# Second experts' rows added into the output by an adding scatter, in place of a scatter, a reload and a gated sum

## The chip, the cores and the metric

One NeuronCore of a Trainium2 chip runs the whole program. The metric is the device time in microseconds of one execution. The engines are TensorE (PE in the profile), VectorE (DVE), ScalarE (ACT), GpSimd (POOL) and SyncE (SP, which only issues DMAs). A row that begins with SPq, ACTq or POOLq is an instruction of that engine's sequencer.

## The reference, cut to what matters

The network has two graph layers and two mixture-of-experts layers over 1250 nodes of 512 features. Only the last layer is touched:

```python
f = layernorm(x)                              # 1250 x 512
logits = f @ Wr                               # 8 experts
top_vals, top_idx = top_k(logits, 2)
gates[n, top_idx[n]] = softmax(top_vals)[n]
for e in range(8):
    y = gelu(f @ W1[e] + b1[e]) @ W2[e] + b2[e]
    out = out + gates[:, e:e+1] * y
result = x + out
```

So each node's result is its row of x plus two expert rows, each times a gate of its own.

## The kernel before, in words

Rows of x are held in the chip's memory as 10 tiles of 125 partitions (node 125 t + p is partition p of tile t). Up to line 1721 the kernel computes x, adds the graph layer to it (line 1340 on POOL, one tile at a time, semaphore `conv_added`), normalises it into `T.rows_b` (line 1713 on ACT, `f_rows`), and turns it for the router's products. SP stores the normalised rows into the DRAM tensor `rows1` in groups of 4, 4 and 2 tiles: the first two groups at line 1272, the last by POOL at line 1342. In `rows1` partition p has its 10 rows next to each other.

DVE then makes the routing (lines 1891 to 1956). The 2500 pairs of node and choice are sorted by expert into blocks of 128 places, 28 blocks at most, and 24 are in use with these inputs. `rows_placed` (803) and L1926 make 0/1 matrices, and PE multiplies them with numbers of nodes (`make_numbers`, 812) and with the choice, first or second (`make_choices`, 820). From these DVE makes `T.ids` (the node of each place, 1937) and `T2.sids` (the row of the DRAM tensor `y1` that each place's result goes to, 1939 to 1943). `keep_busy` (123) issues products whose results nobody uses, 24 of them at 1609 and 24 at 1616.

Then come the blocks, in the functions `block_turn`, `block_hidden`, `turn_hidden`, `block_output`. For block r:

- POOL copies a column of ids (1310) and gathers 128 rows of `rows1` by an indirect DMA (1316), one of 4 buffers. It copies a column of `sids` (1313) and scatters the results of block r-4 into `y1` (1326). It issues these in one order, gather r, then scatter r-4, with a wait for `ry_copied` between.
- PE turns the gathered rows (1527), multiplies with W1 of the block's expert (1535), turns the result (1544), multiplies with W2 (1552). The order on PE is: turn hidden r-1, hidden r, turn of block r+1, output r-1.
- DVE adds b1 (1856), copies the turned rows (1850), adds b2 into `T.ry` (1863), one of 4 buffers.
- ACT takes the gelu (1694) and copies its turned result (1699).

The first 4 blocks and the last 4 stand alone, those between are a loop of 4 to a turn. Scatter r waits only until its buffer's next user is free, so several are in flight. The last 4 count on `ry_last`.

After the last scatter has landed, SP loads `y1` back in 10 DMAs (1277): place p, tile t, first and second choice. DVE does `x = x + gate * row` 20 times (1966, 1968), and ACT stores x into `out` in 10 DMAs (1743) and waits for them. `y1` has rows that no node owns, and lines 880 to 883 fill them once, much earlier, from SP.

Of the kernel before, what the change touches and what calls it, by code (L numbers as in the profile page):

```python
# [815 lines left out]

def make_choices(pe, T, bank, rows, place, columns):
# [52 lines left out]
def projections(nc, T, S, A):  # L870


    with nc.Block() as block:

        @block.sync
        def _(sp):
# [3 lines left out]
            for j in range(TOP):  # L880
                spare = A.y1[j * PLACES + NT * P:(j + 1) * PLACES].rearrange("(p t) d -> p (t d)", t=NT)
                for c0, c1 in ((0, KD * N), (KD * N, NT * D)):
                    sp.dma_start(spare[:, c0:c1], feats[0:128 - P, 0:c1 - c0]).then_inc(S.rows_filled, 16)
            for j in range(TOP):
# [3 lines left out]
            sp.wait_ge(S.rows_filled, 128)  # L888
# [270 lines left out]
def routed_layers(nc, T, T2, S, A):  # L1159
# [62 lines left out]
    with nc.Block() as block:  # L1222

        @block.sync
        def _(sp):
# [55 lines left out]
        @block.gpsimd  # L1281
        def _(pool):
# [59 lines left out]
            pool.dma_start(A.rows1.rearrange("(p t) d -> p t d", t=NT)[:, NT - 2:], T.rows_b[:, NT - 2:]).then_inc(S.tail_stored, 16)  # L1342
            pool.wait_ge(S.ids_ready, 2)
            pool.wait_ge(S.table_made, 2 * TOP)
# [914 lines left out]
```

## Time and profile before

| what | value |
|---|---|
| median of 3 runs | 1360.15 us (1358.65 to 1361.75) |
| profiled execution, its time | 1373.4 us |
| profiled execution, its span | 1371.7 us |
| PE, DVE, ACT, POOL busy | 96%, 54%, 34%, 26% of the span |
| mean granted clock of TensorE | 0.972 |

The span runs from the first to the last instruction of the profiled execution, and all times in rows are microseconds from its start. The profiled execution is 13.25 us (1.0%) above the median. PE's 96% is an average over many stages; it says nothing of the last 25 us, in which PE does nothing.

### The profile page before, as it was taken

What the parts mean: (1) busy time and instruction counts of PE and PEld (TensorE: products, weight loads), DVE (VectorE), ACT (ScalarE), POOL (GpSimd) and SP (SyncE); (2) the same over time, 40 slices, a digit from 0 to 9 for tenths busy, and PEclk for the clock granted to TensorE, in tenths of its full rate; (3) what the DMA queues carried; (4) which work ended last, traced back from release to release, by engine and by line L of the source; (5) the groups of instructions that cost most, each with busy time, mean ns of one, the idle gap of its engine ahead of it and who ended that gap; (6) DMA issues with size and microseconds to landing.
All of it is one profiled execution on the core that took longest, in us unless ns stands there. A gap on an engine that the chain in (4) does not pass through costs nothing.

```text
span 1371.7 us, 23245 instructions
## 1 busy us (share of the span) xinstructions
PE 1316.7 (96%) x7745; PEld 881.9 (64%) x7746; DVE 736.0 (54%) x1600; ACT 461.9 (34%) x1152; POOL 350.6 (26%) x491
## 2 busy tenths in 40 slices
PE   9999999999989999999998999999999999899991
PEld 4799954455457777777656777777645555666660
DVE  6799955562158888887575333333352011453334
ACT  2699921011045555555312111111332012521110
POOL 4499920000000000000033555555200000314540
PEclk9999999999999999999999999999999999769996
DMA  6000000040010000000242999999420070312326
GB/s 166 32 2 3 2 1 1 0 188 0 0 42 2 1 2 2 2 1 2 69 139 85 338 329 319 316 322 311 156 115 0 0 245 0 129 53 88 104 85 237
DMA packets 83549, 133.32 MB, mean 97 GB/s; under 512 B 11952, under 2 KB 49222, under 8 KB 82687
## 3 DMA queue, kind: packets, MB, share of 16 engines
q1 hardware_dynamic: 69491, 110.29, 24.6%
q0 software_dynamic: 12176, 18.68, 4.4%
q10 hardware_dynamic: 1788, 3.16, 0.7%
q8 instruction: 52, 0.85, 0.3%
q14 instruction: 42, 0.34, 0.1%
HBM read 117.41 MB, written 29.56 MB: 107 GB/s over the span
## 4 chain that ended last, share of the span: by engine, by line
PE 45%; DVE 3%; DMA 1%; issue 1%; ACT 0%; SPq 0%; POOL 0%; POOLq 0%; DVEq 0%
PE ps L1377 8%; PE ps L1386 8%; PE ps L1469 6%; PE ps L1535 3%; PE ps L1552 3%; PE ps L1519 2%; PE ps L1514 2%; PE ps L123 2%; PE ps L1367 1%; PE ps L1571 1%; PE ps L1486 1%; PE ps L1412 1%; DMA b_r<-y 1%; PE ps L1527 1%; PE ps L1464 1%; PE ps L164 1%
## 5 line engine op out<-in xcount | busy, mean ns | idle before, releaser
L1298 POOL TENSOR_TENSOR b_x<-b_x,b_r 125x512 f32<-125x512 f32 x10 | 12.7, 1271 | 526.5 <-DVE b_r L1769 526.5
L1377 PEld LDWEIGHTS ps<-b_r 128*128 128x128 f32 x1024 | 124.2, 192 | 33.7 <-issue 32.2
L1377 PE MATMUL ps<-b_r 128*128 128x78 f32 x1024 | 122.2, 272 | 1.2 <-DVE b_r L1751 1.2
L1386 PE MATMUL ps<-b_r 128*78 128x512 f32 x256 | 120.3, 592 | 0.0
L659 PE MATMUL ps<-b_r 125*125 125x160 f32 x660 | 117.3, 314 | 0.1
L568 ACT ACTIVATE b_r<-b_r 125x125 f32<-125x125 f32 x330 | 106.8, 390 | 0.4 <-issue 0.2
L1651 ACT ACTIVATE b_r<-ps,b_r 128x78 f32<-128x78 f32 x128 | 34.8, 323 | 203.0 <-PE ps L1377 196.7
L1047 PEld LDWEIGHTS ps<-b_r 125*64 125x64 f32 x1600 | 85.3, 136 | 24.6 <-issue 22.8
L1010 PE MATMUL ps<-b_r 64*125 64x417 f32 (+1 forms) x480 | 95.7, 531 | 1.4 <-DVE ps L1139 1.2
L1047 PE MATMUL ps<-b_r 125*64 125x125 f32 x1600 | 94.7, 272 | 1.3 <-ACT b_r L1075 1.3
L659 PEld LDWEIGHTS ps<-b_r 125*125 125x125 f32 x660 | 92.0, 187 | 5.4 <-ACT b_r L568 0.2
L1757 DVE COPY b_r<-ps 78x512 f32<-78x512 f32 x64 | 44.0, 687 | 81.1 <-PE ps L1386 78.7
L1469 PE MATMUL ps<-b_r 125*128 125x417 f32 (+1 forms) x240 | 87.3, 513 | 0.0
L676 PE MATMUL ps<-b_r 125*125 125x512 f32 x200 | 86.2, 593 | 0.7 <-DVE b_r L474 0.7
L1292 POOL DMA_INDIRECT y<-b_r,b_affine x64 | 62.0, 969 | 97.1 <-DVE b_r L1757 97.1
L1070 DVE COPY b_r<-ps 125x500 f32<-125x500 f32 x120 | 77.7, 676 | 5.9 <-PE ps L1017 0.7
L1751 DVE COPY b_r<-ps 128x312 f32<-128x312 f32 x64 | 30.9, 483 | 87.4 <-PE ps L1377 52.9
L1286 POOL DMA_INDIRECT b_r<-rows,b_ids x64 | 66.4, 1038 | 28.0 <-issue 18.6
L460 DVE TENSOR_TENSOR b_r<-ps,b_r 125x480 f32<-125x480 f32 x110 | 72.0, 655 | 0.5 <-PE ps L659 0.2
L1083 ACT ACTIVATE b_r<-ps,b_neg_max 125x1251 f32<-125x1251 f32 x40 | 52.2, 1304 | 59.1 <-DVE b_neg_max L1113 55.9
L676 PEld LDWEIGHTS ps<-b_r 125*125 125x125 f32 x200 | 37.4, 188 | 48.3 <-issue 48.3
L1469 PEld LDWEIGHTS ps<-b_r 125*128 125x128 f32 x240 | 44.4, 189 | 36.1 <-issue 35.2
(286 smaller groups left out, 2305.6 us busy)
## 6 DMA issues: line engine op xcount, KB each, us to landing
b_r<-L_ffn_w SPq DMA_DIRECT2D x128, 512.0 KB
b_r<-y SPq DMA_DIRECT2D x20, 512.0 KB, 7.7
b_r<-L_ffn_W SPq DMA_DIRECT2D x2, 4096.0 KB, 20.0
y<-b_r SPq DMA_DIRECT2D x2, 2500.0 KB
rows<-b_r SPq DMA_DIRECT2D x4, 960.0 KB
b_x<-x SPq DMA_DIRECT2D x5, 480.0 KB
out<-b_x ACTq DMA_DIRECT2D x5, 480.0 KB
b_r<-L_ffn_b SPq DMA_DIRECT2D x1, 2048.0 KB, 8.9
```

Source lines behind the costliest of these rows:

```text
L460: dve.tensor_tensor(T.cells[:, b], cell_iota.unsqueeze(1).to_broadcast([EC, CJ, WC]), column(T.cell_col, g, WC), ALU.is_equal).then_inc(S. ...
L568: last = act.activation(T.weighted[:, i % 2, j, :], T.sources[:, i % 2, j, :], ACT.Copy, scale=T.w_col[:, bass.ds(g0 + i, 1), j])
L659: last = pe.matmul(T.ps[:P, 2 + b, 0:WC], T.weighted[:, b, j, :], T.cells[:, b, j, :], start=(j == 0), stop=(j == CJ - 1))
L676: last = pe.matmul(T.ps[:P, t % 2, :], T.at[:, k, t * P:(t + 1) * P], T.rows_a[:, k, :], start=(k == 0), stop=(k == NT - 1))
L1010: last = pe.matmul(T.ps[:P, 3 * h + c, 0:width], T.qt[b:b + DH, m, t * P:(t + 1) * P], T.kt[b:b + DH, m, c0:c0 + width], start=True, stop= ...
L1047: last = pe.matmul(T.ps[b:b + DH, bank_of((VALUES, n)), 0:P], T.v[:, k, m * 128 + b:m * 128 + b + DH], T.probs_t[:, n % 2, h, k * P:(k + 1 ...
L1070: copy(T.probs_t[:, n % 2, h, t * P:(t + 4) * P], bank).then_inc(emptied, 1)
L1286: pool.indirect_dma_start(T.ex[:CAP, e % SLOTS, :], None, A.rows0, bass.IndirectOffsetOnAxis(ap=T.ids[:CAP, e:e + 1], axis=0), bounds_chec ...
L1292: pool.indirect_dma_start(A.y0, bass.IndirectOffsetOnAxis(ap=T.sids[:CAP, e:e + 1], axis=0), T.ey[:CAP, e % SLOTS, :], None, bounds_check= ...
L1377: last = pe.matmul(T.ps[:, 2 + r % 2, f * CAP:(f + 1) * CAP], T.ew1[r % WS][:, k, f * 128:(f + 1) * 128], T.ex_t[:, r % 2, k, :], start=(k ...
L1386: last = pe.matmul(T.ps[:CAP, 4 + r % 2, :], T.eh[:, r % 2, f, :], T.ew2[r % WS][:, f, :], start=(f == 0), stop=(f == FK - 1))
L1469: return pe.matmul(T.ps[:, bank_of(j), 0:n], T.rows_a[:, k, m * 128:(m + 1) * 128], T.ct_f[:, k, c0:c0 + n], start=(k == 0), stop=(k == NT ...
```

## The change

The result of a block is multiplied by its places' gates on DVE, and scattered with an add straight into `out`, which by then holds x. Two choices of one node are in different blocks, and two adds to one row must not overlap, so each scatter waits until the one before it has landed.

- x is stored into `out` by SP, in the same three groups as the normalised rows and between them: x group 0, rows group 0, x group 1, rows group 1, x group 2 (6 DMAs added).
- `rows1` is stored by node number (node 125 t + p at row 125 t + p), so one list of ids serves the gather and the scatter. `make_choices` and four steps of DVE go.
- Gates per place: DVE splits the gates into three bf16 parts (`split_gates`, before the ids), spreads them over the place matrix (`gates_placed`, 3 instructions of 560 elements, after the ids), PE makes 20 products of 84 columns (`make_gates`), DVE adds the parts (`slot_gates`, 3 instructions). PE's second filler is 10, then the gates, then 6, where it was 24.
- In the blocks DVE has one more instruction, a multiplication of 128x512 in place, which waits for the one before it (`ry_copied`), and POOL waits for `ry_scaled`, then for the landing of the scatter before.
- The reload, DVE's 20 instructions and ACT's 10 stores at the end go, as do the four fills of `y1`. SP waits for the last scatters at the end.
- The place matrices move from region r1 to r2, so that they outlive the first gathers.

```diff
-            for j in range(TOP):
-                spare = A.y1[j * PLACES + NT * P:(j + 1) * PLACES].rearrange("(p t) d -> p (t d)", t=NT)
-                for c0, c1 in ((0, KD * N), (KD * N, NT * D)):
-                    sp.dma_start(spare[:, c0:c1], feats[0:128 - P, 0:c1 - c0]).then_inc(S.rows_filled, 16)
...
-            for t0, n in GROUPS[:2]:
+            for t0, n in GROUPS:
+                sp.wait_ge(S.conv_added, t0 + n)
+                for p0, p1 in ((0, 120), (120, P)):
+                    sp.dma_start(A.out.rearrange("(t p) d -> p t d", t=NT)[p0:p1, t0:t0 + n], T.x[p0:p1, t0:t0 + n])\
+                      .then_inc(S.out_stored, 16)
+                if t0 + n == NT:
+                    break
                 sp.wait_ge(S.f_rows, t0 + n)
                 for p0, p1 in ((0, 120), (120, P)):
-                    sp.dma_start(A.rows1.rearrange("(p t) d -> p t d", t=NT)[p0:p1, t0:t0 + n], T.rows_b[p0:p1, t0:t0 + n])\
+                    sp.dma_start(A.rows1.rearrange("(t p) d -> p t d", t=NT)[p0:p1, t0:t0 + n], T.rows_b[p0:p1, t0:t0 + n])\
                       .then_inc(S.rows_stored, 16)
+            sp.wait_ge(S.out_stored, 96)
             sp.wait_ge(S.ry_last, 64)
-            for i in range(NT // 2):
-                for j, rows in enumerate((T.all_a, T.all_d)):
-                    sp.dma_start(rows[:, 2 * i:2 * i + 2],
-                                 A.y1[j * PLACES:(j + 1) * PLACES].rearrange("(p t) d -> p t d", t=NT)[:, 2 * i:2 * i + 2])\
-                      .then_inc(S.y_gathered[i], 16)
...
-                if r + 1 < 8:
-                    wait_count(pool, S.ry_stored[(r + 1) % 4], q, 16, 16 * ((r + 1) // 4))
-                pool.wait_ge(S.ry_copied, q * 4 + (r + 1))
+                pool.wait_ge(S.ry_scaled, q * 4 + (r + 1))
+                if r > 4:
+                    pool.wait_ge(S.ry_last, 16 * (r - 4))
+                else:
+                    wait_count(pool, S.ry_stored[(r + 3) % 4], q, 16, 16 if r > 0 else 0)
                 place_column(q, r + 1, (r + 1) % 4 if r + 1 < 8 else 4)
-                pool.indirect_dma_start(A.y1, bass.IndirectOffsetOnAxis(ap=T.ey_ids[:, r % 4:r % 4 + 1], axis=0),
-                                        T.ry[:, r % 4, :], None, bounds_check=TOP * PLACES - 1, oob_is_err=False)\
+                pool.indirect_dma_start(A.out, bass.IndirectOffsetOnAxis(ap=T.ey_ids[:, r % 4:r % 4 + 1], axis=0),
+                                        T.ry[:, r % 4, :], None, bounds_check=N - 1, oob_is_err=False, compute_op=ALU.add)\
                     .then_inc(stored, 16)
...
-            pool.wait_ge(S.table_made, 2 * TOP)
             token_column(0, 0)
...
-            make_choices(pe, T2, 3, BR, T2.place, NB).then_inc(S.table_made, 1)
-            keep_busy(pe, T, 0, 24)
+            keep_busy(pe, T, 0, 10)
+            pe.wait_ge(S.gates_ready, 2)
+            make_gates(pe, T2, 5).then_inc(S.table_made, 1)
+            keep_busy(pe, T, 0, 6)
...
+                dve.wait_ge(S.ry_copied, q * 4 + (r + 1))
+                dve.tensor_scalar(T.ry[:, r % SLOTS1, :], T.ry[:, r % SLOTS1, :], T2.slot_gate[:, bass.ds(q * 4 + r, 1)], None,
+                                  ALU.mult).then_inc(S.ry_scaled, 1)
...
             gates(dve, link, T)
+            split_gates(dve, link, T2)
             dve.wait_ge(S.table_made, 1 + TOP)
...
+            link(dve.tensor_scalar(T2.sids[:, 0:NB], T.ps[:BR, 7, 0:NB], float(N), None, ALU.add))
             dve.tensor_copy(T.ey_ids[:, 0:1], T2.sids[:, 0:1])
+            gates_placed(dve, T2, S.gates_ready)
...
             block_turned(0, 0)
+            dve.wait_ge(S.table_made, 2 + TOP)
+            slot_gates(dve, link, T2, 5)
             end = blocks(dve, block_step)
             block_output(*end)
-
-            rows = (T.rows_a, T.rows_d)
-            for t in range(NT):
-                dve.wait_ge(S.y_gathered[t // 2], 64)
-                link(dve.scalar_tensor_tensor(out=T.x[:, t, :], in0=rows[0][:, t, :], scalar=T.gate[:, t, 0:1],
-                                              in1=T.x[:, t, :], op0=ALU.mult, op1=ALU.add))
-                dve.scalar_tensor_tensor(out=T.x[:, t, :], in0=rows[1][:, t, :], scalar=T.gate[:, t, 1:2],
-                                         in1=T.x[:, t, :], op0=ALU.mult, op1=ALU.add).then_inc(S.out_ready, 1)
```

The new functions:

```python
def split_gates(dve, link, T):
    rest = T.gate[:]
    for i in range(3):
        link(dve.tensor_copy(T.split[:, i], rest))
        if i < 2:
            link(dve.tensor_tensor(T.rest[:], rest, T.split[:, i], ALU.subtract))
            rest = T.rest[:]

def gates_placed(dve, T, ready):
    for i in range(3):
        last = dve.tensor_tensor(T.gate_parts[:, :, :, i, :], T.place[:],
                                 T.split[:, i].rearrange("p t j -> p j t").unsqueeze(3).to_broadcast([P, TOP, NT, NB]), ALU.mult)
    last.then_inc(ready, 1)
```

## Rows read from the trace of the kernel before

**Rows 1.** Windows of the block stage, of the reload's start and of the end.
```profile
core 0: us, PE busy (x) PEld busy (x) DVE busy (x) ACT busy (x) POOL busy (x), PEclk, DMA share, GB/s
1232.00:1345.00 113.00, 106.67 (x442) 69.45 (x439) 41.22 (x72) 19.27 (x48) 56.49 (x93) 1.00 0.28 91
1345.00:1352.00 7.00, 0.00 (x0) 0.00 (x0) 0.00 (x0) 0.00 (x0) 0.67 (x1) 0.50 0.57 197
1352.00:1372.00 20.00, 0.00 (x0) 0.00 (x0) 14.41 (x20) 0.00 (x0) 0.00 (x0) 0.50 0.86 323
```

**Rows 2.** The chain that ended last, its last pieces: start, us, what.
```profile
1336.06 1.99 PE ps L1535 x8
1340.56 1.99 PE ps L1552 x4
1344.68 2.28 DMA y<-b_r
1351.76 12.88 DMA b_r<-y
```

**Rows 3.** Timeline of the last block: start, us, instruction, idle before it.
```profile
1341.59 0.99 POOL L1326 DMA_INDIRECT y<-b_r  x1 [0.55 <-issue]
1342.69 0.69 DVE L1863 TENSOR_TENSOR b_r<-ps,b_r 128x512 f32<-128x512 f32 x1 [2.08 <-PE ps L1552]
1343.93 0.18 POOL L1313 COPY b_r<-b_r 128x1 int32 x1 [1.36 <-DVE b_r L1863]
1344.68 0.99 POOL L1326 DMA_INDIRECT y<-b_r  x1 [0.57 <-issue]
1346.98 5.33 SPq L1277 DMA_DIRECT2D b_r<-y  x10
```

**Rows 4.** The scatters of the block stage, by line: durations, first and last start, landing.
```profile
L1326 POOL DMA_INDIRECT y<-b_r x24: 982/1026/1035, 1245.4 to 1344.7; - x24
DMA to landing us min/median/max: 2.1/2.5/2.8
```

**Rows 5.** Windows around the last scatter, then around a gather issued at 1239.05.
```profile
1344.68:1345.67 0.99, 0.00 (x0) 0.00 (x0) 0.00 (x0) 0.00 (x0) 0.99 (x1) 0.63 0.00 0
1345.67:1346.20 0.53, 0.00 (x0) 0.00 (x0) 0.00 (x0) 0.00 (x0) 0.00 (x0) 0.50 0.00 0
1346.20:1347.00 0.80, 0.00 (x0) 0.00 (x0) 0.00 (x0) 0.00 (x0) 0.00 (x0) 0.50 0.16 47
...
1239.05:1240.70 1.65, 1.33 (x7) 1.13 (x7) 0.00 (x0) 0.38 (x1) 1.02 (x1) 1.00 0.00 0
1240.70:1241.40 0.70, 0.70 (x6) 0.57 (x5) 0.00 (x0) 0.00 (x0) 0.00 (x0) 1.00 0.44 118
1241.40:1242.15 0.75, 0.75 (x7) 0.51 (x6) 0.56 (x2) 0.10 (x1) 0.00 (x0) 1.00 0.08 33
```

**Rows 6.** DVE in a middle block, from the timeline, and normalisation's multiply by line.
```profile
1327.21 0.69 DVE L1863 TENSOR_TENSOR b_r<-ps,b_r 128x512 f32<-128x512 f32 x1 [1.15 <-issue]
1329.41 0.42 DVE L1856 TENSOR_TENSOR b_r<-ps,b_w_b 128x256 f32<-128x256 f32 x1 [1.51 <-PE ps L1535]
...
L216 DVE TENSOR_SCALAR b_r<-b_x,b_moments,b_rstd x30: 545/545/547, 7.9 to 1039.1; 125x512 f32<-125x512 f32 x30
```

**Rows 7.** Timeline of the routing on DVE, PE and POOL.
```profile
1223.05 0.81 DVE L1926 TENSOR_TENSOR b_r<-b_block_iota,b_keep 125x280 f16<-125x280 f32 x2
1227.25 0.17 DVE L710 TENSOR_TENSOR b_gate<-b_gate,b_gap 125x10 f32<-125x10 f32 x1
1228.63 0.19 DVE L1937 TENSOR_SCALAR b_ids<-ps 128x28 int32<-128x28 f32 x1 [1.21 <-PE ps L812]
1228.62 5.34 PE L123 MATMUL ps<-b_ones_bf 125*128 125x512 bf16 x24
1230.37 1.10 POOL L1316 DMA_INDIRECT b_r<-rows,b_ex_ids  x1 [0.92 <-issue]
1234.01 0.63 PE L1527 MATMUL ps<-b_ident,b_r 128*128 128x128 f32 x4
```

**Rows 8.** Windows between the stores of rows1 and the first gather.
```profile
1199.00:1210.00 11.00, 11.00 (x49) 9.61 (x49) 3.16 (x11) 3.24 (x7) 0.63 (x1) 0.50 0.50 126
1216.00:1220.00 4.00, 4.00 (x37) 4.00 (x37) 2.19 (x17) 0.21 (x1) 0.00 (x0) 0.50 0.00 0
1234.00:1236.00 2.00, 1.01 (x6) 0.76 (x7) 0.69 (x1) 0.00 (x0) 1.02 (x3) 1.00 0.68 213
```

**Rows 9.** SP's waits over the whole run: us in total, times, longest.
```profile
SPq L873 <- PEq L873: 86.6, 1, 86.6
```

More of the change, by code:

```diff
@@ L814, in make_numbers, with make_gates, slot_gates @@
     return last
+def split_gates(dve, link, T):
+    rest = T.gate[:]
+    for i in range(3):
+        link(dve.tensor_copy(T.split[:, i], rest))
+        if i < 2:
+            link(dve.tensor_tensor(T.rest[:], rest, T.split[:, i], ALU.subtract))
[4 more added lines that the diff above has]
+                                 T.split[:, i].rearrange("p t j -> p j t").unsqueeze(3).to_broadcast([P, TOP, NT, NB]), ALU.mult)
+    last.then_inc(ready, 1)
+def make_gates(pe, T, bank):
+    for t in range(NT):
+        for j in range(TOP):
+            last = pe.matmul(T.ps[:BR, bank, 0:3 * NB], T.place_rows[:, t * TOP + j, :],
+                             T.gate_parts[:, j, t].rearrange("p i b -> p (i b)"),
+                             start=(t + j == 0), stop=(t == NT - 1 and j == TOP - 1))
+    return last
+def slot_gates(dve, link, T, bank):
+    part = [T.ps[:BR, bank, i * NB:(i + 1) * NB] for i in range(3)]
+    link(dve.tensor_copy(T.slot_gate[:], part[2]))
+    link(dve.tensor_tensor(T.slot_gate[:], part[1], T.slot_gate[:], ALU.add))
+    link(dve.tensor_tensor(T.slot_gate[:], part[0], T.slot_gate[:], ALU.add))
 def make_choices(pe, T, bank, rows, place, columns):
@@ L887, in _ @@
                     sp.dma_start(filled[:, c0:c1], feats[:, 0:c1 - c0]).then_inc(S.rows_filled, 16)
[L888 removed]
+            sp.wait_ge(S.rows_filled, 64)
         @block.tensor
@@ L1341, in _ @@
             pool.wait_ge(S.f_rows, NT)
-            pool.dma_start(A.rows1.rearrange("(p t) d -> p t d", t=NT)[:, NT - 2:], T.rows_b[:, NT - 2:]).then_inc(S.tail_stored, 16)
+            pool.dma_start(A.rows1.rearrange("(t p) d -> p t d", t=NT)[:, NT - 2:], T.rows_b[:, NT - 2:]).then_inc(S.tail_stored, 16)
             pool.wait_ge(S.ids_ready, 2)
-            pool.wait_ge(S.table_made, 2 * TOP)
             token_column(0, 0)
@@ L1350, in _ @@
             pool.wait_ge(S.blocks_ready, 1)
+            pool.wait_ge(S.out_stored, 96)
             loops = loops_of(pool)
@@ L1737, in _ @@
             block_turned(*end)
-            out = A.out.rearrange("(t p) d -> p t d", t=NT)
-            for i in range(NT // 2):
-                act.wait_ge(S.out_ready, 2 * i + 2)
-                for p0, p1 in ((0, 120), (120, P)):
-                    act.dma_start(out[p0:p1, 2 * i:2 * i + 2], T.x[p0:p1, 2 * i:2 * i + 2]).then_inc(S.out_stored, 16)
-            act.wait_ge(S.out_stored, 16 * NT)
         @block.vector
@@ L1890, in _ @@
             one, other = T.expert_iota[:, 0:E1].unsqueeze(1), T.expert_iota[:, 0:E1].unsqueeze(2)
-            link(dve.scalar_tensor_tensor(out=T2.place_number, in0=T.part_number[:].to_broadcast([P, NT]), scalar=float(NT),
-                                          in1=T.tile_iota[:], op0=ALU.mult, op1=ALU.add))
-            link(dve.tensor_scalar(T2.place_number, T2.place_number, float(NOWHERE - N), None, ALU.add))
+            link(dve.scalar_tensor_tensor(out=T2.place_number, in0=T.tile_iota[:], scalar=float(P),
+                                          in1=T.part_number[:].to_broadcast([P, NT]), op0=ALU.mult, op1=ALU.add))
+            link(dve.tensor_scalar(T2.place_number, T2.place_number, float(EMPTY - N), None, ALU.add))
             dve.memset(T2.sids[:, NB:], 0)
@@ L1935, in _ @@
             gates(dve, link, T)
+            split_gates(dve, link, T2)
             dve.wait_ge(S.table_made, 1 + TOP)
             dve.tensor_scalar(T.ids[:, 0:NB], T.ps[:BR, 7, 0:NB], float(N), None, ALU.add).then_inc(S.ids_ready, 1)
-            low, place = T.ids_low[:, 0:NB], T2.place_ids[:, 0:NB]
-            link(dve.tensor_scalar(low, T.ps[:BR, 7, 0:NB], float(N), None, ALU.add))
-            link(dve.tensor_scalar(place, low, float(N), float(TOP * PLACES), ALU.is_ge, ALU.mult))
-            link(dve.tensor_tensor(place, place, low, ALU.add))
-            dve.wait_ge(S.table_made, 2 * TOP)
-            link(dve.scalar_tensor_tensor(out=T2.sids[:, 0:NB], in0=T.ps[:BR, 3, 0:NB], scalar=float(PLACES), in1=place,
-                                          op0=ALU.mult, op1=ALU.add))
+            link(dve.tensor_scalar(T2.sids[:, 0:NB], T.ps[:BR, 7, 0:NB], float(N), None, ALU.add))
             dve.tensor_copy(T.ey_ids[:, 0:1], T2.sids[:, 0:1])
+            gates_placed(dve, T2, S.gates_ready)
             last_block = T.first_block[:P, E1:E1 + 1]
```

13 lines of the change are left out of this document (8 added, 5 removed).

## The prediction

> **What bounds the kernel now.** The windows come first, because the page's 96% for PE is an average. In the block stage PE is busy 106.67 of 113 us at the full clock (1.00, the 2.4 GHz level), and from 1345 to the end it does nothing [rows 1]. So two stages matter: one in which PE sets the pace, and one in which only DVE and DMAs work. The chain that ended last says the same: PE's products up to 1342.54, then the last scatter, then 12.88 us of reloads and what follows them [rows 2]. The last scatter is issued at 1344.68, and 2.28 us later SP's reload starts, at 1346.98 [rows 2, 3]. The span ends at 1371.7. The tail after the last landing is therefore 1371.7 - 1347.0 = 24.7 us. All 24 scatters start between 1245.4 and 1344.7, and the first 23 of them take 1341.59 - 1245.4 = 96.2 us, 4.37 us from one to the next [rows 3, 4]. That is PE's pace. The last gap is 3.09 us, since PE has no further block by then [rows 3].
>
> **What goes.** The reload, the 20 gated sums and the stores: all of the 24.7 us, in which nothing else runs. The four fills of y1 save nothing: SP waited 86.6 us for PE at the end of that stage, so four DMAs fewer leave it waiting longer [rows 9].
>
> **The stores of x.** Six more DMAs, 2.5 MB, go through SP's queue ahead of and between the stores of normalised rows, and the first gather has to wait for the latter. The stores of rows1 moved 126 GB/s over 11 us up to 1210, in a stage where engines and not DMAs set the pace; 2.5 MB at that rate take 20 us. Group 0 of x is ready when POOL has added four tiles, long before its normalised rows, and the stretch from 1216 to 1220 has no DMA at all [rows 8]. The gather is issued at 1230.37 [rows 7]. I cost the stores at nothing; the cover is that idle stretch. If they were late, the gather would slip by what is left of them, a few us at most. The new order in rows1 keeps the bytes and makes pieces of 2 KB out of 8 KB; the same cover holds.
>
> **The routing.** DVE gets five linked steps of some 0.2 us each before the ids (the last step of the gates takes 0.17), 1.05 us in all, and it sat idle 1.21 us there for PE [rows 7]. So they fit with nothing much to spare; I take +0.1 us. After the ids, four steps go (0.9 us with their gaps) and one comes (0.2). The three spreads of 560 elements are priced from the 280-element comparison, 0.405 us each: at most twice that, 0.8 us, so 2.4 us together [rows 7]. The gates' products can start near 1231.5. PE's filler of 10 takes 10 x 0.222 = 2.2 us (24 took 5.34) from about 1228.4, PE idles about 1 us, the 20 products take about 1 us, the filler of 6 takes 1.3: PE is free at 1233.8, where before it was at 1233.96 [rows 7]. The first gather lands some 3 us after its issue anyway. Net: 0 to +0.3, I take +0.1. DVE's list of block experts is ready near 1232.7, before the first turn at 1234.01. `slot_gates` (3 x 0.2 us) fits behind the first copy, while PE makes the first hidden product.
>
> **The blocks on DVE.** The multiplication costs 0.55 us, the time of the 125x512 row that also multiplies by a column (a lower price is possible with one operation less, none below 0), and 0.05 for its wait: 0.6 us. It stands between L1863, which ends at 1327.90, and L1856 at 1329.41, an idle of 1.51 us [rows 6]. PE waits for `ry_copied`, which comes before it. So it costs PE nothing and makes each scatter ready 0.6 us later. The first is issued at 1245.4 + 0.6 = 1246.0.
>
> **One scatter at a time.** This decides the change. POOL now waits for the landing of the scatter before, copies a column and issues. From the start of that copy to the next scatter it takes 0.75 us (1343.93 to 1344.68), and I add 0.2 for POOL waking before the copy, 0.95 us [rows 3]. With L for the time from an adding scatter's issue to its landing, one scatter follows another at L + 0.95 at the soonest. PE's pace of 4.37 hides that up to L = 3.42. Above it, a chain from the first scatter sets the end: last issue = 1246.0 + 23 (L + 0.95), last landing L later, and about 0.6 us to the span's end. **End = 1268.4 + 24 L.** Each tenth of a us in L is 2.4 us.
>
> No row shows an adding DMA, so L is bounded from its parts. A plain scatter lands after 2.1 to 2.8 us, the last one after 2.28 [rows 2, 4]; adding can't be quicker, as it writes the same rows and reads more. That is the lower end, 2.3. In the windows the scatter moves nothing for 1.5 us and then works for 0.8; a gather, which reads such rows from DRAM, moves nothing for 1.6 us and then works for up to 1.4 [rows 5]. If an adding scatter did the whole of a gather and then the whole of a scatter's part behind the issue (2.5 - 1.0 = 1.5), it would be 3.1 + 1.5 = 4.6, and with the longest scatter and some more for the issue of extra descriptors 5.0. That is the upper end. I take 1.6 us to the first packet, 1.2 for the reads at a gather's pace and 0.7 for the writes at a scatter's: L = 3.5, nearer to the lower end because reads and writes of different rows can overlap.
>
> The Trainium skill (DMA: Bandwidth & Descriptors, "Two DMAs through the same engine are not ordered") says that only the completion semaphore orders a DMA behind one that writes what it reads; it is why the wait is there, and it speaks against this change. The same page ("Anatomy of one DMA — SWDGE (gpsimd) path") puts about 2.0 us plus bytes / 436e3 on a DMA; for 256 KB that is an estimate of 2.6 us, near the rows' 2.5, and by it alone the add would be hidden.
>
> **The sum.** End = 1268.4 + 24 x 3.5 = 1352.4, plus 0.1 for the routing: 1352.5 against 1371.7, a gain of 19.2 us. The profiled execution lies 1.0% above the median of the runs; I take the same gain off the median: 1360.15 - 19.2 = **1341.0 us**.
>
> **Rivals.**
>
> *All of it hidden.* If only the data phase grows by the 0.7 us of a second read, L is 3.1 and PE keeps the pace. The last scatter but one goes out at 1342.2, the last at 1342.2 + 3.1 + 0.95 = 1346.3, and the end is at 1350.0, a gain of 21.7: 1338.5 us. With L = 2.3 the gain is 23.4 and the time 1336.8. For it: the plain scatter's 16 queues work for only 0.8 us. Against: the gather's reads are slower than the scatter's writes in the same windows. The Trainium skill (Collectives: The Full Stack, "The bandwidth ceiling: the fold count and why AG ≠ RS ≠ AR") holds that an adding DMA is slower because of its two source reads and not because of the add; that is this case.
>
> *The chain of landings becomes the bound and eats the gain.* Place: POOL's wait for the landing before L1313's copy. It decides from L = 4.30, where 1268.4 + 24 L is 1371.7. At the upper end of 5.0 the end is at 1388.4, 16.7 us later: 1376.9 us. Gathers then queue behind the waiting POOL and PE starves at POOL's pace. For it: reads of DRAM followed by writes of the same rows leave no room for overlap within a row, and the descriptors of an add may take POOL longer than 1.0 us to issue. Against: eight rows per queue can follow each other. This is the case on the other side.
>
> *The clock.* PE's filler is shorter and has a gap of about 1 us. If the granted clock fell to 0.50 there, some 4 us of PE's work would take twice as long, +2 us. Against: it held 1.00 in a stretch of which PE worked only 1.01 of 2.00 us [rows 8]. It changes no sign.
>
> **How the numbers follow.** A measurement of this kernel can tell about 0.2% (2.7 us) from no change. In L the bounds of "same" are 4.19 and 4.41. Chances: L up to 3.2, all hidden, 0.24 (1337 to 1339); L from 3.2 to 4.19, the forecast's case, 0.42 (1339 to 1357); L within the bounds of "same", 0.07; L above, 0.27 (1363 to 1377 and more). That makes faster 0.66, same 0.07, slower 0.27. The range takes both ends of L: 1336 from the plain scatter's time, and 1377 from 5.0. The forecast's side alone is 1336 to 1357.
>
> **What would show it.** In the profile after: the landing of the adding scatters by line (3.5 us); their distance from one to the next (4.45, against 4.37); POOL's wait before L1313's counterpart put down to a DMA and not to DVE; the span ending within 1 us of the last landing; the first turn of block 0 within 0.3 us of 1234.0; the clock at 1.00 from 1226 on; DVE's multiplication at 0.55 us with PE's time per block unchanged. It is wrong if the landing is above 4.3 us, or if PE's first turn slips by more than 1 us.

## The result, and the profile after

The change makes the kernel slower: 1373.93 us (median of 4 runs, 1371.46 to 1381.96) against 1360.95 (4 runs, 1358.65 to 1362.24), a ratio of 1.0109 with a 95% interval of [1.0071, 1.0146]. A second measurement gave 1371.49 (13 runs) against 1361.46 (23 runs), 1.0059 [1.0036, 1.0083]. So it costs 10 to 13 us where 19 were forecast to be won. 1373.9 lies inside the range of 1336 to 1377, but on the other side of no change from the forecast of 1341.0, in the part that the second rival held.

TensorE's mean granted clock differs from one execution to the next, in both kernels: the profiled execution of before was at 0.972, the first profiled one of the changed kernel at 0.985, its second (the same kernel, experiment 8) at 0.977. In both kernels an execution with the lower mean (0.972 to 0.974 before, 0.977 changed) takes some 12 us more than the others, and the profile of before is one of these. The windows show where. First the kernel before, then the changed kernel's first and second execution; the third figure from the end is the granted clock:

```profile
1190.00:1200.00 10.00, 10.00 (x46) 9.21 (x45) 4.50 (x18) 4.79 (x10) 0.00 (x1) 0.50 0.42 109
1200.00:1210.00 10.00, 10.00 (x44) 8.61 (x43) 3.16 (x11) 3.24 (x7) 0.63 (x1) 0.50 0.47 119
1210.00:1225.00 15.00, 14.44 (x74) 10.84 (x74) 9.62 (x62) 3.36 (x9) 0.00 (x0) 0.50 0.03 12
```

```profile
1190.00:1200.00 10.00, 9.84 (x80) 8.13 (x79) 7.17 (x28) 7.40 (x16) 0.00 (x0) 1.00 0.89 259
1200.00:1210.00 10.00, 8.46 (x72) 7.06 (x72) 6.44 (x53) 2.14 (x4) 1.23 (x1) 0.79 0.44 139
1210.00:1225.00 15.00, 12.63 (x87) 6.48 (x86) 10.99 (x37) 3.71 (x11) 5.85 (x9) 0.91 0.19 55
```

```profile
1190.00:1200.00 10.00, 10.00 (x47) 9.30 (x46) 4.11 (x17) 4.42 (x9) 0.00 (x0) 0.50 0.72 210
1200.00:1210.00 10.00, 10.00 (x45) 8.61 (x43) 3.16 (x11) 3.23 (x7) 1.23 (x1) 0.50 0.54 144
1210.00:1225.00 15.00, 14.44 (x73) 10.57 (x73) 10.04 (x63) 3.77 (x11) 0.00 (x0) 0.50 0.08 27
```

Before and the second execution both did these 35 us at 0.50, the 1.2 GHz level; the first did most of them at 1.00. I therefore set the second execution (span 1382.2, time 1383.92) against the profile of before (span 1371.7, time 1373.4). That is 10.5 us, as the medians say, and the stages in front of the change hardly differ. In the first execution the first scatter is issued at 1234.1 and not at 1245.5; these 11 us go with the clock and not with the change. What makes the clock come out one way or the other isn't shown.

The scatters by tile, second execution (durations, first and last start, who waited, landing), with two windows, from the first scatter to the last and from there to the end:

```profile
L1362 POOL DMA_INDIRECT out<-b_r x24: 1563/1594/1636, 1245.5 to 1375.2; - x24
who waited for it (us, times):
  POOL b_r L1347: 42.7, 21
DMA to landing us min/median/max: 3.4/4.8/5.0
```

```profile
1245.50:1375.24 129.74, 98.96 (x384) 59.91 (x382) 50.12 (x89) 17.59 (x44) 65.33 (x84) 0.97 0.41 70
1375.24:1382.20 6.96, 0.00 (x0) 0.00 (x0) 0.00 (x0) 0.00 (x0) 1.56 (x1) 0.50 0.05 7
```

Against [rows 1, 4]: an issue takes 1.59 us where it took 1.03, a landing 4.8 where it took 2.5, and between first and last scatter PE works 98.96 of 129.74 us, so it is no longer the bound. (The 2.5 is the median of the only four landings that the trace of before has, and two of these blocks were nearly empty; the other two landed after 2.7 to 2.8 us.) The chain that ended last says what is: from 1245.48 on its long pieces are landings of this kind, with POOL's copy and issue between them, and its last piece is POOL's closing drain. Three of these pieces:

```profile
1341.98 4.97 DMA out<-b_r
1369.17 4.76 DMA out<-b_r
1375.02 1.79 POOLq L1254
```

The timeline of POOL and of the engines that feed it, same execution, one block:

```profile
1341.98 1.59 POOL L1362 DMA_INDIRECT out<-b_r  x1 [0.59 <-POOL b_r L1347]
1343.94 1.06 POOL L1350 DMA_INDIRECT b_r<-rows,b_ex_ids  x1 [0.16 <-issue]
1345.96 0.49 DVE L1897 TENSOR_SCALAR b_r<-b_r 128x512 f32<-128x512 f32 x1
1347.17 0.18 POOL L1347 COPY b_r<-b_r 128x1 int32 x1 [2.17 <-DMA out<-b_r]
1347.94 1.60 POOL L1362 DMA_INDIRECT out<-b_r  x1 [0.59 <-POOL b_r L1347]
1348.07 0.66 PE L1563 MATMUL ps<-b_ident,b_r 128*128 128x128 f32 x4 [1.23 <-DMA b_r<-rows,b_ex_ids]
```

The scaled rows were ready at 1346.45, 0.5 us before the scatter of 1341.98 landed (at 1346.95). POOL starts its copy 0.22 us after that landing and the next scatter 0.77 later, 5.96 us behind the last. The gather stands behind the scatter in POOL's queue, so PE waits 1.23 us for gathered rows and works at POOL's pace.

The description of the kernel before says that several of its scatters are in flight. They may be, but [rows 4] shows that they weren't: they were issued 4.3 us apart and landed within 2.8.

**The balance**, predicted and measured, in us of these executions:

| term | before | predicted | measured |
|---|---|---|---|
| first scatter issued at | 1245.4 | 1246.1 | 1245.5 |
| first to last scatter, 23 distances | 99.3 | 102.4 (4.45 each) | 129.8 (5.64 each) |
| last scatter to the end of the span | 27.0 | 4.1 | 6.9 |
| span | 1371.7 | 1352.5 | 1382.2 |

The tail gives 20.1 us back and the distances take 30.5, 10.5 in all with the 0.1 of the first term. Of the error of 29.7 us, 27.4 lie in the distances and 2.8 in the end; the first scatter came 0.6 earlier than forecast.

**The end** is a part of its own. The closing drain, an instruction with which each engine ends the program, is no busy time; it stands by the line of the block that ends the program. In the kernel before, then in the changed kernel's first execution (with what SP did) and its last scatter from POOL's timeline:

```profile
L1222 POOLq DRAIN  x1: 6353/6353/6353, 1344.5 to 1344.5; - x1
```

```profile
L1254 POOLq DRAIN  x1: 6932/6932/6932, 1362.6 to 1362.6; - x1
L1254 SPq DRAIN  x1: 13/13/13, 1366.4 to 1366.4; - x1
L1254 SPq EVENT_SEMAPHORE  x1: 17/17/17, 1369.7 to 1369.7; - x1
```

```profile
1362.78 1.56 POOL L1362 DMA_INDIRECT out<-b_r  x1 [0.89 <-issue]
```

SP saw the last landing and was through at 1366.4; then all waited 3.3 us for POOL. The last scatter's issue ends at 1362.78 + 1.56 = 1364.34, and the drain at 1362.56 + 6.93 = 1369.49, 5.14 us behind it. In the kernel before it ended 5.14 us behind the end of the last issue as well (1345.67, 1350.81), but there it lay beside the reload and cost nothing. The change took that cover away.

### The profile page after: what moved, and what is told of

It reads as the page before. It is cut to its first block, busy times and chain, and to the rows that moved or that the text cites. A ratio compares the mean times of both kernels' runs of the same rounds, so it can differ in the third digit from the quotient of the medians.

```text
span 1369.7 us, 23259 instructions
## 1 busy us (share of the span) xinstructions
PE 1306.6 (95%) x7747; PEld 870.3 (64%) x7748; DVE 736.9 (54%) x1612; ACT 461.2 (34%) x1152; POOL 366.5 (27%) x491
## 4 chain that ended last, share of the span: by engine, by line
PE 35%; DMA 8%; DVE 4%; issue 2%; POOL 1%; ACT 1%; POOLq 0%; DVEq 0%
PE ps L1413 8%; PE ps L1422 8%; DMA out<-b_r 7%; PE ps L1505 6%; PE ps L1555 2%; PE ps L1550 2%; PE ps L1403 1%; PE ps L1522 1%; PE ps L1448 1%; PE ps L1439 1%; PE ps L1500 1%; PE ps L123 1%; DVE b_stats L200 1%; PE ps L144 1%; DMA b_r<-rows,b_ex_ids 1%
## 6 DMA issues: line engine op xcount, KB each, us to landing
b_r<-L_ffn_W SPq DMA_DIRECT2D x2, 4096.0 KB, 20.1
```

## Experiments

Twelve runs: eleven edits of the changed kernel, and the changed kernel itself again. Where "one execution" is said, the time is a single one and says little within some us. "Distance" is the mean of the 23 from first to last scatter in the profiled execution, "end" is from the last scatter's issue to the span's end.

### 1. The scatter without its add

```diff
-                    T.ry[:, r % 4, :], None, bounds_check=N - 1, oob_is_err=False, compute_op=ALU.add)\
+                    T.ry[:, r % 4, :], None, bounds_check=N - 1, oob_is_err=False)\
```

> The changed kernel with a plain scatter in place of the adding one; every wait stays. The rows of x are overwritten, so the output leaves out the sum. Theory (the landing of the adding scatter is the cost: 4.8 us from issue to landing, 5.8 us from one scatter to the next): a plain scatter lands after about 2.5 us, the chain asks for 3.4 us, PE's 4.37 us sets the pace again, and the time falls by about 24 x 1.4 = 33 us, to some 1340 us. Rival (the longer routing, the multiplication on DVE, the stores of x or the wait itself cost the time, whatever lands): the distance between scatters stays near 5.8 us and the time near 1372 us. Second rival (the issue of 1.6 us on POOL is the cost, and it is the same with indices into the output): the issue stays at 1.6 us.

1339.13 us (ratio to before 0.9833 [0.9777, 0.989]).

```profile
L1362 POOL DMA_INDIRECT out<-b_r x24: 985/1021/1034, 1235.7 to 1331.9; - x24
DMA to landing us min/median/max: 2.1/2.8/3.3
```

Distance 4.18, end 6.4, issue 1.0: the theory held against both rivals. Everything else of the change is in this kernel: the stores of x between those of the rows, the gates, the wait for each landing. So these together cost next to nothing, and the add costs 32 to 35 us. The time is also within a us of what the first rival gave for a hidden landing (1338.5), but in part by luck: in this execution the end is 2.7 us longer than that rival had it (3.7), and the distances together are 4.1 us shorter (96.2 against 100.3).

### 2. The column copied before the waits

```diff
+                place_column(q, r + 1, (r + 1) % 4 if r + 1 < 8 else 4)
                 pool.wait_ge(S.ry_scaled, q * 4 + (r + 1))
...
-                place_column(q, r + 1, (r + 1) % 4 if r + 1 < 8 else 4)
+                pool.sem_inc(S.pool_go, 1)
```

The last line counts up a semaphore that nobody waits for; the wait for the landing stands at this instruction.

> POOL copies the column of places before it waits for the landing, not between landing and issue. Theory: the distance between scatters is landing plus 0.95 us now and becomes landing plus about 0.3 us, so 23 x 0.65 = 15 us go: 1358 us, level with the kernel before. Rival (POOL's own work of gather, copies and issue sets the pace, and the order of its steps doesn't matter): the distance stays within 0.1 us of 5.8 and the time within 3 us of 1373.

1370.49 us (1.0074 [1.0037, 1.011]), 1 to 3 us less than the changed kernel where 15 were expected: a miss. The rival, that POOL's own work sets the pace, isn't borne out either: experiment 3 has the same work and a distance of 4.2.

```profile
1256.46 1.60 POOL L1363 DMA_INDIRECT out<-b_r  x1 [2.57 <-DMA out<-b_r]
1262.09 1.59 POOL L1363 DMA_INDIRECT out<-b_r  x1 [2.39 <-DMA out<-b_r]
```

The distance is 5.54 against 5.6, though no copy stands between landing and issue. From a landing to the next issue it is 0.84 to 0.90 us here and was 0.93 to 1.01 with the copy (1.32 at the last scatter). So nearly all of it is POOL's own way from a semaphore to a started indirect DMA, and the copy, which takes 0.18, runs mostly inside it. My theory had the 0.65 us as the copy's.

### 3. Two chains

Even blocks add into `out`, odd ones into a second tensor, and a scatter waits for the one before last. The sum of the two tensors is left out.

```diff
-                if r > 4:
-                    pool.wait_ge(S.ry_last, 16 * (r - 4))
+                if r > 5:
+                    pool.wait_ge(last_of[r % 2], 16)
...
-                    wait_count(pool, S.ry_stored[(r + 3) % 4], q, 16, 16 if r > 0 else 0)
+                    wait_count(pool, S.ry_stored[(r + 2) % 4], q, 16, 16 if r > 1 else 0)
...
-                pool.indirect_dma_start(A.out, ...
+                pool.indirect_dma_start((A.out, A.y1)[r % 2], ...
```

> Blocks of even number add into the output, blocks of odd number into a second tensor, and each scatter waits for the one before the last. The odd blocks' sums are left out of the output. Theory (latency of one scatter behind another): two may be in flight, a chain asks for (4.8 + 0.95) / 2 = 2.9 us per block, PE sets the pace at 4.37 us and the time is near 1340 us. Rival (the adding scatters are bound by what the queues can do at all, so two in flight take twice as long each): landings of 7 us or more, a distance of over 5 us and a time over 1355 us.

1337.88 us (0.9826 [0.9772, 0.9881]). From the DMA view (issues, median us to landing):

```profile
out<-b_r POOLq DMA_INDIRECT x12, 4.8
y<-b_r POOLq DMA_INDIRECT x12, 4.8
```

The kernel is as quick as without the add. The adds' work isn't the bound, nor is their issue of 1.6 us; waiting for one before the next is. How far two adds can share the DMA engines is not shown: the distance here is 4.2 us, and a scatter's data moves from 2.1 to 4.5 us behind its issue (windows under "Why the prediction was wrong"), so one add has moved its data before the next begins.

### 4 and 5. Half the columns, half the places

```diff
-                pool.indirect_dma_start(A.out, bass.IndirectOffsetOnAxis(ap=T.ey_ids[:, r % 4:r % 4 + 1], axis=0),
-                                        T.ry[:, r % 4, :], None, bounds_check=N - 1, oob_is_err=False, compute_op=ALU.add)\
+                pool.indirect_dma_start(A.half, bass.IndirectOffsetOnAxis(ap=T.ey_ids[:, r % 4:r % 4 + 1], axis=0),
+                                        T.ry[:, r % 4, 0:D // 2], None, bounds_check=N - 1, oob_is_err=False, compute_op=ALU.add)\
```

```diff
-                pool.indirect_dma_start(A.out, bass.IndirectOffsetOnAxis(ap=T.ey_ids[:, r % 4:r % 4 + 1], axis=0),
-                                        T.ry[:, r % 4, :], None, bounds_check=N - 1, oob_is_err=False, compute_op=ALU.add)\
+                pool.indirect_dma_start(A.out, bass.IndirectOffsetOnAxis(ap=T.ey_ids[0:64, r % 4:r % 4 + 1], axis=0),
+                                        T.ry[0:64, r % 4, :], None, bounds_check=N - 1, oob_is_err=False, compute_op=ALU.add)\
```

> The adding scatter takes 256 of 512 columns, into a tensor of rows of 1 KB; the output leaves the sums out. Theory (the time behind the issue is that of the bytes read and written): issue stays at 1.6 us, the 3.2 us behind it fall by about 1.1 us, landing at 3.7 us, and the chain at 4.65 us. Rival (a cost per row, whatever its length): landing stays at 4.6 us or more, and the time near 1370 us.

> The adding scatter takes 64 of a block's 128 places, whole rows of 2 KB; the other places are left out of the output. Theory (behind the issue the time is that of the rows moved, and the issue itself is per row): issue near 1.0 to 1.3 us, and a landing near 3.3 us, below the 3.8 us of half-length rows because descriptors go as well. Rival (issue is a fixed cost of the adding form): issue stays 1.6 us and landing 3.8 us.

One execution each: 1352.47 us and 1351.0. The scatters of the first, then of the second:

```profile
L1362 POOL DMA_INDIRECT half<-b_r x24: 1563/1600/1775, 1235.1 to 1343.8; - x24
DMA to landing us min/median/max: 2.9/3.8/4.0
```

```profile
L1362 POOL DMA_INDIRECT out<-b_r x24: 1422/1458/1648, 1237.4 to 1342.4; - x24
DMA to landing us min/median/max: 2.9/3.6/3.8
```

Half the bytes take 1.0 us off the landing, half the places 1.2, and the issue keeps 1.46 us for 64 places. So, as an estimate from these two, about 2 to 2.4 us of the 4.8 grow with the bytes and 2.4 to 2.8 don't. The theory for half the columns held (3.7 expected); for half the places it didn't: the issue hardly fell (1.0 to 1.3 expected), and the landing lies nearer to the rival's 3.8 than to 3.3. The distances are (1343.8 - 1235.1) / 23 = 4.73 and 4.57, the landing plus 0.9 to 1.0 in both.

### 6. Waiting by expert

Two adds can meet in one row only if their blocks belong to different experts, for a node chooses an expert once. DVE compares the blocks' experts and writes 0 or 16 for each; POOL loads it and waits for the scatter before only where the expert changes and for every fourth block, else for the one before that.

```diff
-                if r > 4:
-                    pool.wait_ge(S.ry_last, 16 * (r - 4))
+                if r > 0:
+                    other = pool.value_load(T.other[0:1, bass.ds(q * 4 + r, 1)], min_val=0, max_val=16)
+                    pool.wait_ge(S.ry_stored[(r - 1) % 4], q * 16 + 16 * ((r - 1) // 4) + other)
                 else:
-                    wait_count(pool, S.ry_stored[(r + 3) % 4], q, 16, 16 if r > 0 else 0)
+                    pool.wait_ge(S.ry_stored[3], q * 16)
+                pool.wait_ge(S.ry_stored[(r - 2) % 4], q * 16 + 16 * ((r - 2) // 4 + 1))
...
+            for slot in range(4):
+                pool.wait_ge(S.ry_stored[slot], loops * 16 + 32)
...
+            dve.memset(T.same_f[0:1, 0:1], 0.0)
+            link(dve.tensor_tensor(T.same_f[0:1, 1:NB], T.block_expert_f[0:1, 1:NB], T.block_expert_f[0:1, 0:NB - 1], ALU.is_equal))
+            dve.tensor_scalar(T.other[0:1, :], T.same_f[0:1, :], -16.0, 16.0, ALU.mult, ALU.add)
```

SP's wait for the last scatters (`ry_last`) goes; POOL waits for them at its end.

> Two blocks of one expert never hold the same node. DVE makes a table that says for each block whether its expert differs from the one before, and the scatter waits for the landing before it only then (and for every fourth block); otherwise for the one before that. Nothing is left out. Theory (only waiting for landings costs the time): where two may be in flight PE's pace of 4.37 us holds, at a change of expert 1.4 us are lost and made up behind it; 1340 to 1346 us, 16 to 22 us below the kernel before. Rival (the remaining full waits, about half of the 24, hold the chain back as they come too close): 1350 to 1360 us.

1349.34 us (0.9889 [0.985, 0.9927]): it beats both kernels, but by less than the theory had (1340 to 1346), and the time lies just under the rival's 1350 to 1360. Four scatters from its timeline show what is left:

```profile
1310.16 1.60 POOL L1363 DMA_INDIRECT out<-b_r  x1 [0.59 <-POOL b_r L1346]
1315.94 1.59 POOL L1363 DMA_INDIRECT out<-b_r  x1 [0.59 <-issue]
1321.46 1.60 POOL L1363 DMA_INDIRECT out<-b_r  x1 [0.59 <-POOL b_r L1346]
1324.86 1.59 POOL L1363 DMA_INDIRECT out<-b_r  x1 [0.17 <-POOL b_r L1346]
```

A full wait makes a distance of 5.5 to 6.0, and where POOL catches up the distance is 3.4 at the least, as long as it also issues a gather for each block. From first to last scatter it is 104.7 us.

### 7. The stores of x all behind those of the rows

```diff
+            for t0, n in GROUPS[:2]:
+                sp.wait_ge(S.f_rows, t0 + n)
+                for p0, p1 in ((0, 120), (120, P)):
...
-                if t0 + n == NT:
-                    break
-                sp.wait_ge(S.f_rows, t0 + n)
...
```

> The six stores of x come behind those of the normalised rows on SP's queue, not between them. Theory (the stores are hidden either way): first gather, first turn and the time as in the changed kernel, within 3 us of 1373. Rival (their place matters): the first gather or the first adding scatter shifts by more than 1 us and the time with it.

1374.78 us (1.0092 [1.0062, 1.0123]), against 1371.49 (1.0059 [1.0036, 1.0083]) of the changed kernel beside it: the intervals overlap, and the order brings nothing. In its profile the first gather is issued at 1220.9 against 1218.1 in the changed kernel's first execution, more than the 1 us that the rival asked for; but the granted clock from 1210 to 1225 was 0.83 there and 0.91 here, so this pair of profiles doesn't tell the order from the clock.

### 8. The changed kernel again

> The changed kernel itself, for a comparison on one chip with e7 and e6. 1372 to 1375 us, about 12 us above the kernel before. Executions with a granted clock near 0.975 should be some 10 us longer than those near 0.986 in this kernel as in the kernel before, if the clock in the routing stage is what lay between the profiled execution of before and its median.

1371.49 us (1368.9 to 1383.92), of 13 executions, just under the 1372 to 1375 expected and 10 us above the kernel before. The longest is the one at 0.977, 12 us above the median; the others, at 0.982 to 0.989, take 1369 to 1375. So the clock part of the expectation held, on one execution at the low value (and one of 1381.96 at 0.977 in the first measurement). Its profile stands above.

### 9, 10 and 11. What is left in the version by expert

9 moves the wait for the last four landings from POOL's end to DVE's (the lines added in the first diff are DVE's); 10 also frees the fourth blocks; 11 also loads the value before the wait for the rows. Each cut is shown against the version before it.

```diff
-            for slot in range(4):
-                pool.wait_ge(S.ry_stored[slot], loops * 16 + 32)
+            for slot in range(4):
+                dve.wait_ge(S.ry_stored[slot], end[0] * 16 + 32)
+                dve.memset(T.same_f[0:1, slot:slot + 1], 0.0)
```

```diff
-                    pool.wait_ge(S.ry_stored[3], q * 16)
+                    full = pool.value_load(T.full[0:1, bass.ds(q * 4, 1)], min_val=0, max_val=4 * NB)
+                    pool.wait_ge(S.ry_stored[3], full)
```

```diff
-                pool.wait_ge(S.ry_scaled, q * 4 + (r + 1))
...
+                pool.wait_ge(S.ry_scaled, q * 4 + (r + 1))
```

> The by-expert version with one thing moved: POOL no longer waits for the last four landings, DVE does. Found in its trace: POOL's closing drain ran 5.12 us after the last landing, and nothing beside it; in the changed kernel it started 0.2 us before the last scatter's issue and took 6.93 us, so it ended 3.3 us after the landing, and the span with it. Theory (the drain is behind POOL's last instruction, so it can run beside the landing): the span ends 6.9 us after the last scatter is issued, not 9.2, 2.3 us sooner: about 1346 to 1347. Rival (the drain only ends after the DMAs it issued have landed, plus some 5 us): no change, 1349.

> As the one above, and the full wait for the scatter before goes also for every fourth block where its expert is that of the block before: full waits at the 7 changes of expert alone. In the by-expert trace a block with a full wait comes 5.5 to 6.0 us after the one before it, one with a free wait behind it 3.4 to 3.6, and undisturbed ones 4.65; from first to last scatter it took 104.7 us, against 96 to 97 at PE's pace. Theory (the full waits are what is left of the loss): first to last is 99 to 101 us, the time 1341 to 1344. Rival (POOL's own work per block, two indirect DMAs and the loads from the table, or the longer landing of two adds in flight, sets the distance): 104 us stays, and the time is that of the kernel above, 1346 to 1347.

> As the version with full waits at the changes of expert alone, but POOL loads its wait's value before it waits for the block's scaled rows, not behind. In that version's trace the load and its arithmetic take 0.79 us (once 1.4) between the rows being ready and the wait for the landing, in each block. Theory (that is on the path wherever the scatter before has already landed, the last four blocks among them): first to last scatter falls from 102.6 to about 100 us, the time from 1349.5 to about 1347. Rival (blocks with a full wait set the distance, and there the load is beside the landing): no change, 1349 to 1350.

| kernel | time | ratio to before | first to last scatter | end |
|---|---|---|---|---|
| 6 | 1349.34 | 0.9889 [0.985, 0.9927] | 104.7 | 9.4 |
| 9 | 1351.59 | 0.9936 [0.9909, 0.9962] | 105.2 | 6.9 |
| 10 | 1349.5 | 0.9907 [0.9871, 0.9943] | 102.6 | 6.9 |
| 11 | 1344.6 | 0.99 [0.9874, 0.9927] | 99.6 | 6.9 |

Kernel 9's end is shorter by 2.5 us (2.3 expected), but its time isn't: the two intervals overlap, and I can't say where the rest went. Kernel 10 wins 2.6 us between the scatters where I had expected 4 to 6, and at 1349.5 it missed the 1341 to 1344 of the theory. That its waits are at the changes of expert alone is therefore worth little by itself. Its undisturbed distances were still 4.6, and kernel 11 shows why: with the load moved ahead of the wait they are 4.3 to 4.4, and the time is 1344.6 where 1347 was expected. First, the scatters and POOL's waits in 11:

```profile
L1366 POOL DMA_INDIRECT out<-b_r x24: 1563/1596/1750, 1233.8 to 1333.4; - x24
DMA to landing us min/median/max: 3.3/4.9/5.2
POOL b_r L1346 <- DMA out<-b_r: 12.9, 7, 2.1
```

Seven waits for a landing, one for each change of expert, cost 12.9 us of POOL's time, where 21 cost 42.7, and first to last is 99.6 us, what it was before the change (99.3). The median is 1344.6 against 1360.25 in the same measurement, 15.7 us less; the ratio's interval says 0.7 to 1.3% quicker than the kernel before, which is 10 to 17 us.

### 12. POOL waits for the last landing too

```diff
+            pool.wait_ge(S.ry_last, 64)
```

The line is POOL's last.

> The changed kernel with one line more: POOL too waits for the landing of the last scatter before it ends. It tells whether POOL's closing drain is what the span's end hangs on. Theory (the drain takes about 5.1 us from the landing on, where it took 6.93 us from 0.2 us before the issue on): from the last scatter's issue to the span's end it is landing (3.4, since the last block has few valid places) + 0.9 + 5.3 = 9.5 us against 6.9 in the changed kernel. Rival (SP's wait for the landing sets the end): 6.9 us or less.

One execution, 1372.63 us.

```profile
1361.69 1.56 POOL L1362 DMA_INDIRECT out<-b_r  x1 [0.90 <-issue]
L1254 POOLq DRAIN  x1: 5130/5130/5130, 1365.5 to 1365.5; - x1
```

The span ends at 1370.9, 9.2 us behind the last issue against 6.9 in the changed kernel; 9.5 was expected. The drain takes 5.1 us even if POOL's DMAs have all landed. In the ten profiled executions of the changed kernel and its variants in which POOL doesn't wait at its end (experiment 5's issue is shorter), and in the kernel before and experiment 1 with their plain scatters, it ends 5.14 us behind the end of POOL's last issue, though it begins anywhere from 0.2 to 0.5 us before that issue. The span ends 0.23 us later, unless other work follows. So the end is issue + 5.14 + 0.23: 6.9 us with an issue of 1.56, 6.8 in experiment 5 with 1.42, 6.4 in experiment 1 with 0.99. The landing of the last scatter has no part in it.

## Why the prediction was wrong, and where it was right

**The step that failed** is "I take 1.6 us to the first packet, 1.2 for the reads at a gather's pace and 0.7 for the writes at a scatter's: L = 3.5". Measured, L is 4.8: the size of this term was wrong, and with it the side on which the chain of landings fell. Windows around an adding scatter issued at 1356.67, landing at 1361.46, when nothing else ran (first execution): until its data moves, while it moves, until it lands.

```profile
1356.67:1358.80 2.13, 0.00 (x0) 0.00 (x0) 0.00 (x0) 0.00 (x0) 1.56 (x1) 0.50 0.00 0
1358.80:1361.14 2.34, 0.00 (x0) 0.00 (x0) 0.00 (x0) 0.00 (x0) 0.00 (x0) 0.50 0.90 112
1361.14:1361.46 0.32, 0.00 (x0) 0.00 (x0) 0.00 (x0) 0.00 (x0) 0.00 (x0) 0.50 0.00 0
```

The same for a plain scatter in the kernel before, issued at 1341.59, and the working stretch of a gather issued at 1321.29:

```profile
1341.59:1343.14 1.55, 0.95 (x3) 0.12 (x1) 0.45 (x1) 0.00 (x0) 0.99 (x1) 1.00 0.00 0
1343.14:1344.00 0.86, 0.00 (x0) 0.00 (x0) 0.24 (x1) 0.00 (x0) 0.07 (x1) 1.00 0.78 305
1344.00:1344.33 0.33, 0.00 (x0) 0.00 (x0) 0.00 (x0) 0.00 (x0) 0.12 (x1) 1.00 0.00 0
1323.05:1324.50 1.45, 1.45 (x8) 1.27 (x8) 0.27 (x1) 0.15 (x1) 0.38 (x2) 1.00 0.66 192
```

Nothing moves for 2.1 us (forecast 1.6), and the 0.6 above the plain scatter's 1.55 is what the issue itself takes longer (1.56 against 0.99). The queues then work for 2.34 us, where I had 1.2 + 0.7 = 1.9. A plain scatter of the same 262 KB works for 0.86 and a gather for 1.45 (some other packets share its window), 2.31 together: the measured time is that of the one and then the other, with no overlap to be seen. And 0.32 us pass from the last data to the landing, as in the plain scatter, for which the forecast's sum had no term. The argument that "reads and writes of different rows can overlap" put L nearer to the lower end, with nothing in the trace for it. The sum of a gather's and a scatter's parts, 4.6, was in the text and would have been right within 0.2.

The windows of [rows 5] were a weak base for these parts. The scatter of 1344.68 moved 47 GB/s x 0.80 us = 38 KB and the gather of 1239.05 some 107 KB, where a full block has 262 KB. That a full block's scatter and gather work about as long as I read there, 0.86 and 1.45 us, is luck.

The Trainium skill (Collectives: The Full Stack, "The bandwidth ceiling: the fold count and why AG ≠ RS ≠ AR") says of a ring's ReduceScatter that it is slower because the add needs two source reads, and not because the add costs cycles. Carried over to this scatter, it would double the working phase, an estimate of 0.86 to 1.7 us; here it is 2.34, 2.7 times as long. So it gives the direction and over half of the size. The Trainium skill's fit (DMA: Bandwidth & Descriptors, "Anatomy of one DMA — SWDGE (gpsimd) path") gives an estimate of 2.6 us for this size. The plain scatter of a full block landed after 2.7 to 2.8 us and agrees; the adding one is 2.2 us above it, so the fit doesn't hold for one that adds.

**The formula** held in its form. With L = 4.8, 1268.4 + 24 L is 1383.6, and the span of the second execution is 1382.2. That it comes so near is partly luck: the distances are 2.5 us less than 23 x 5.75 (scatters of blocks with few valid places land after 3.4 us), the first scatter is 0.5 earlier, and the end is 1.5 more than L + 0.6. The pace of "L + 0.95" stands: from a landing to the next issue it is 0.93 to 1.01 us in the changed kernel (1.32 at the last scatter). With the measured end the break-even moves from an L of 4.30 to one near 4.2 (an estimate: the 99.3 + 27.0 us of before less 0.1 and 6.9, by 23, less 0.97). The range of L reached to 5.0 and so held the result; what was wrong is that 0.27 stood on the part above 4.41, where the nearest sum of rows (4.6) lay.

**The tail.** "About 0.6 us to the span's end" after the last landing was wrong as well: 2.8 us too little in the balance. POOL's drain, hidden under the reload in the kernel before, sets the end. What the change removes was worth 20.1 us and not 22.9 at L = 3.5. I had asked of each edit what covers it, but not of the removed reload what it covered.

**What was right.** The stores of x are hidden: the first gather is issued at 1229.66 where it was at 1230.37 [rows 7], and experiment 1, which has them, is quick. The routing, second execution, from the timeline:

```profile
1229.66 1.36 POOL L1350 DMA_INDIRECT b_r<-rows,b_ex_ids  x1 [0.23 <-issue]
1228.65 2.04 DVE L830 TENSOR_TENSOR b_r<-b_r 125x560 bf16<-125x560 f16 x3
1230.74 0.92 PE L839 MATMUL ps<-b_r 125*128 125x84 bf16 x20 [0.42 <-DVE b_r L830]
1233.45 0.63 PE L1563 MATMUL ps<-b_ident,b_r 128*128 128x128 f32 x4 [0.48 <-DMA b_r<-rows,b_ex_ids]
```

The spreads took 2.04 us (2.4 forecast), the gates' products 0.92 (1). From the first gather to the first turn it is 3.79 us against 3.64 [rows 7]. But the first turn, forecast at 1234.0 within 0.3 and 0.1 later than before, came at 1233.45, 0.56 earlier, because the gather did; why is open, and it is small. The clock stayed at 1.00 there (1226 to 1235), so the rival of a falling clock didn't come about in the routing. In the blocks it stayed at 1.00 in the second execution too; in the first it fell to 0.77 from 1330 to 1334, behind 8 us in which PE worked 5.9. DVE's multiplication took 0.49 us (0.55) and cost PE nothing, for in experiment 1, which has it, the distance is 4.18.

## What to carry to other kernels

An adding scatter from POOL is a thing of another class than a plain one: 4.8 us against 2.8 for 128 rows of 2 KB, and a chain of them, each waiting for the last, goes at the landing plus 0.9 to 1.0 us. Use it where the next need not wait for the landing of the last, and ask of the data which pairs can really meet: waiting for the scatter before at 7 of 23 places, and not at all 23, together with the load ahead of the wait and the last wait moved to DVE, turned a loss of 10 us into a gain of 10 to 17. And when a tail is removed, look up what ended underneath it, POOL's drain among it.

## What the runs showed of the hardware that I had not expected

- An adding scatter of 262 KB keeps the DMA queues at work for 2.34 us, as long as a gather (1.45) and a plain scatter (0.86) of that size one behind the other.
- Adding scatters 4.2 us apart (experiment 3) land after 4.8 us each, as in a chain. Closer ones, 3.4 to 3.6 us apart in experiment 11, landed after 4.8 to 5.2. Two full ones whose data moves at the same time were in no run.
- The issue of an adding scatter takes 1.59 us for 128 places and 1.46 for 64, a plain one's 1.02 for 128.
- POOL needs 0.84 to 0.90 us from a landing that it waits for to a started indirect DMA (experiment 2), and with a small copy in between 0.93 to 1.01.
- POOL's closing drain ends 5.14 us behind the end of POOL's last DMA issue, plain or adding, or takes 5.1 us where POOL has waited for all landings; it doesn't wait for the landing itself.
- A gather issued some 2 us behind an adding scatter lands after 4.0 us in the median, behind a plain one after 3.4 (experiment 1).
- PE's distance between blocks was 4.18 in experiment 1 and 4.37 before, with the same products, and in neither does PE's list of waits have more than one wait for another engine there; what makes these 0.19 us wasn't tried.
